# Three-layer graph network with routed feed-forward on one core: surplus pass reordered by its dependences, a second bank for the layer product, and the norm taken tile by tile

## What is computed

```
norm = deg[src]**-0.5 * deg[dst]**-0.5      # edges and self loops
h = layernorm(x)                            # x: 6250 x 256, fp32
for W, b in three layers:
    h = segment_sum((h @ W)[src] * norm, dst) + b     # relu after the first two
x = x + h
n = layernorm(x);  r = n @ wr + br
out = x + n
chosen = the 3124 of 6250 rows with the highest r
out[chosen] += r[chosen] * (gelu(n[chosen] @ w1 + b1) @ w2 + b2)
```

## Time and profile before

| | |
|---|---|
| three runs | 2053.6, 2049.27, 2052.75 us, median 2052.75 |
| profiled execution | 2062.73 us, span 2061.0 us |
| mean granted TensorE clock | 0.959 of full |
| PE busy | 1861.0 us of the span, 90% |
| first sum of layer 2 / of layer 3 (DVE) | 964 us / 1464 us |
| end of the last unit | 1858.6 us |
| PE's last matmul ends | 2051.7 us |

### The profile page before, as it was taken

One profiled execution on the slowest core, in us unless ns is written; L12 is line 12 of the kernel. 1 busy time (PEld: TensorE's weight loads), 2 busy tenths in 40 slices (PEclk: granted clock), 3 DMA queues, 4 the chain that ended last, 5 costly groups with the idle time before them and its releaser, 6 DMA issues.

```text
span 2061.0 us, 28897 instructions
## 1 busy us (share of the span) xinstructions
PE 1861.0 (90%) x10168; PEld 1068.9 (52%) x10168; DVE 1054.3 (51%) x3267; ACT 528.7 (26%) x1126; POOL 1161.9 (56%) x1213
## 2 busy tenths in 40 slices
PE   6874789998899999988999999998899989999898
PEld 5762456665555556543445554544444434446665
DVE  7877688886566566631222221210345444786422
ACT  5824134333344455510211111110000000002120
POOL 5400674666676667523677777762477767762211
PEclk9965899999999999999999999999999999999999
DMA  7649143544455556574667766764588869854200
GB/s 255 195 168 306 40 153 122 178 152 153 158 196 184 178 196 208 193 266 146 212 224 242 239 229 224 233 238 154 205 301 306 308 214 332 312 183 145 63 24 24
DMA packets 170597, 405.02 MB, mean 197 GB/s; under 512 B 29436, under 2 KB 122546, under 8 KB 157657
## 3 DMA queue, kind: packets, MB, share of 16 engines
q1 hardware_dynamic: 119864, 265.05, 36.4%
q0 software_dynamic: 50592, 138.13, 21.2%
HBM read 284.18 MB, written 118.89 MB: 196 GB/s over the span
## 4 chain that ended last, share of the span: by engine, by line
PE 67%; POOL 10%; issue 9%; DVE 7%; DMA 5%; ACT 2%; POOLq 0%; DVEq 0%; ACTq 0%
PE ag L1246 21%; PE pw L1246 16%; PE ag L1258 9%; POOL space_rows L1835 6%; PE pw L1214 5%; PE both L1272 4%; PE pw L1340 3%; PE ag L1353 2%; PE pw L1353 2%; PE ag L1340 1%; PE both L1264 1%; POOL space_rows L1802 1%; POOL space_rows L1827 1%; DMA space_rows<-row_dram,src_s 1%; DMA extra<-space_tables 1%
## 5 line engine op out<-in xcount | busy, mean ns | idle before, releaser
L1835 POOL DMA_INDIRECT space_rows<-row_dram,src_s x947 | 967.9, 1022 | 378.7 <-issue 207.7
L1246 PE MATMUL ag<-space_a,space_ring 128*128 128x512 f16 x2107 | 628.9, 382 | 30.5 <-POOL space_ring L1843 30.5
L1214 PE MATMUL pw<-space_tables 128*128 128x147 f16 (+1 forms) x2022 | 330.1, 248 | 51.5 <-DVE space_tables L871 43.0
L1258 PE MATMUL ag<-space_rows,hots 128*128 128x512 f16 x947 | 359.6, 380 | 5.1 <-DMA space_rows<-row_dram,src_s 3.3
L1214 PEld LDWEIGHTS pw<-space_tables 128*128 128x128 f16 x2022 | 218.9, 116 | 238.5 <-DVE space_tables L871 68.8
L871 DVE TENSOR_TENSOR space_tables<-iota_two,space_tables 128x294 f16<-128x294 f16 (+1 forms) x1011 | 306.6, 338 | 0.0
L1582 ACT ACTIVATE space_ring<-pw 128x784 f16<-128x784 f32 (+1 forms) x257 | 220.1, 857 | 312.3 <-PE pw L1214 308.5
L1246 PEld LDWEIGHTS ag<-space_a,space_ring 128*128 128x128 f16 x2107 | 198.9, 98 | 133.5 <-issue 27.3
L868 DVE TENSOR_TENSOR space_tables<-iota_many,space_tables 128x512 f16<-128x512 f16 x506 | 215.2, 425 | 59.1 <-PE pw L1214 56.5
L1246 PE MATMUL pw<-space_b,space_ring 128*128 128x512 f16 x784 | 204.4, 381 | 6.4 <-DVE space_work L895 6.4
L1246 PE MATMUL pw<-space_a,space_ring 128*128 128x512 f16 x686 | 172.0, 381 | 1.9 <-DVE space_b L895 1.9
(11 more groups left out here) (407 smaller groups left out, 1926.8 us busy)
## 6 DMA issues: line engine op xcount, KB each, us to landing
space_ring<-adj SPq DMA_DIRECT2D x49, 1568.0 KB, 7.5
adj<-space_ring SPq DMA_DIRECT2D x34, 1568.0 KB, 6.2
space_tables<-adj SPq DMA_DIRECT2D x17, 1568.0 KB
extra<-hots SPq DMA_DIRECT2D x3, 6272.0 KB, 23.2
space_work<-extra SPq DMA_DIRECT2D x147, 128.0 KB
space_rows<-row_dram,src_s POOLq DMA_INDIRECT x947, 3.7
space_b<-in_x_turned SPq DMA_DIRECT2D x7, 896.0 KB, 13.6
space_a<-in_x SPq DMA_DIRECT2D x7, 896.0 KB, 5.4
```

Of the source, the lines that this page charges most:

```text
L1214: pe.matmul(pw[v % 2][:, half, at_c:at_c + n], olo[:, j % RING // 2, :, j % 2 * 2 + i], ohi[:, j % RING, 0:n, i], start=s == FIRST[w], sto ...
L1246: mm = pe.matmul(bank(q), a[:, k, :], hh[l][:, k, :], start=i == 0 and not own, stop=i == TILES - 1)
L1258: pe.matmul(bank(q), hots_area[:, hot_at, :, g - SPOT_GROUPS[SPOT_GROUP_OF[g]][0]], slots[g % GR], start=False, stop=i == n).then_inc(g_us ...
L1835: pool.indirect_dma_start(slots[g % GR], None, row_dram[STEP_LAYER[g]], bass.IndirectOffsetOnAxis(src_s[:, s:s + 1], 0)).then_inc(g_in[g % ...
```

## The change

- `spill`: the edges are requested, then the target index is computed and the old sum requested with a semaphore of its own (`old_in`); then the wait for the edges, the wait for `rows_out[l]`, the request of the source rows (`more_rows_in`), and the one-hot computed after that. Behind ACT's copy POOL waits only for `old_in`.
- The 8 row steps ahead of `spill(1)` and `spill(2)` are fetched behind them. `SPILL_AT` of these stands 20 units earlier, `OVER_AT` (and with it the first sums of a layer) 30 units earlier.
- The product of layers two to three goes into `pw[1][:, 1]`; its turns wait for ACT's copy of the tile before (`relued`), no more for `lo_s`.
- The norm's statistics are taken with each sum; variance at `NORM_AT`, reciprocal 4 units later, tile i of the group at 6(i+1) units behind `NORM_AT`. `aggr` and `rstd_x` have two buffers.
- The last group of four tiles becomes one of three and one of one; the one tile has an own slot of `xn`.
- Phase two of the choice: the turns' settles stand ahead of its begin, its steps start 3 places earlier at a spacing of 3.8 instead of 4, and the turns of the second block stand one step earlier.

```
 LAG = 5
-AHEAD = 8
...
 BN = 6
-NORMS = (7, 7, 7, 7, 5, 5, 7, 4)
+NORMS = (7, 7, 7, 7, 5, 5, 7, 3, 1)
...
 END = [max(u for u, (p, i) in enumerate(UNIT) if p == q) + 1 for q in range(len(Q))]
-SPILL_AT = [END[0], START[TILES] + 170, START[2 * TILES] + 170]
-OVER_AT = [SPILL_AT[0] + 45, SPILL_AT[1] + 60, SPILL_AT[2] + 60]
+SPILL_AT = [END[0], START[TILES] + 150, START[2 * TILES] + 150]
+OVER_AT = [SPILL_AT[0] + 45, SPILL_AT[1] + 50, SPILL_AT[2] + 50]
...
 SPOTS = by_unit([STEP_UNIT[a] - 60 for a, b in SPOT_GROUPS])
+NORM_SPACE = 6
+XN_FROM = [0] * (len(NORMS) - 1) + [NORMS[-2]]
+NORM_TILE = [(g, i) for g, n in enumerate(NORMS) for i in range(n)]
+NORM_TILE_AT = [NORM_AT[g] + NORM_SPACE * (i + 1) if g < len(NORMS) - 1 else NORM_AT[g] for g, i in NORM_TILE]
+NORM_TILES_OF = by_unit(NORM_TILE_AT)
+ROOTED_OF = by_unit([u + 4 if g < len(NORMS) - 1 else u for g, u in enumerate(NORM_AT)])
...
 def turn_places():
-    hidden = {(0, 4 + i): [s] for i, s in enumerate(BLOCKS[1])} | {(SECOND, 2 + i): [s] for i, s in enumerate(BLOCKS[SECOND + 1])}
+    hidden = {(0, 3 + i): [s] for i, s in enumerate(BLOCKS[1])} | {(SECOND, 2 + i): [s] for i, s in enumerate(BLOCKS[SECOND + 1])}
...
-CHOICE_BEGINS, CHOICE_SPACE = 17.0, 4.0
+CHOICE_BEGINS, CHOICE_SPACE = 14.0, 3.8
...
     both = ps("both", [P, 2 * D])
-    px, ph = both[:, 0:D], both[:, D:2 * D]
+    px = both[:, 0:D]
+    ph = [both[:, D:2 * D], pw[1][:, 1, 0:D]]
...
+            def spread_of_tile(k):
+                (g, i), t = NORM_TILE[k], Q[2 * TILES + k]
+                chained(dve.bn_stats(stats[:, i, :], nodes[:, t]))
+                chained(dve.bn_aggr(aggr[:, g % 2, i, :], stats[:, i, :]))
+
+            def spread_of_group(g):
                 n = NORMS[g]
...
+                chained(dve.tensor_scalar(rstd_x[:, g % 2, 0:n], aggr[:, g % 2, 0:n, 1], EPS, None, ALU.add))
+                steps[f"spread {g}"] = done_x["n"]
+
+            def rooted_group(g):
+                n = NORMS[g]
+                dve.wait_ge(root_s, g + 1)
+                chained(dve.reciprocal(rstd_x[:, g % 2, 0:n], rstd_x[:, g % 2, 0:n]))
+
+            def norm_tile(k):
+                (g, i), t = NORM_TILE[k], Q[2 * TILES + k]
+                if i == 0 and 0 < g <= EARLY_GROUPS:
+                    dve.wait_ge(pairs_out, 48 * NORM_FROM[g])
+                elif i == 0 and g and not XN_FROM[g]:
+                    dve.wait_ge(pairs_late, 48 * (NORM_FROM[g] - EARLY))
+                to = xn[:, XN_FROM[g] + i]
+                chained(dve.tensor_scalar(to, nodes[:, t], aggr[:, g % 2, i, 0:1], rstd_x[:, g % 2, i:i + 1], ALU.subtract, ALU.mult))
+                dve.tensor_tensor(nodes[:, t], nodes[:, t], to, ALU.add).then_inc(norm_s, 1)
+                dve.scalar_tensor_tensor(x_junk, to, 1.0, wr_b, ALU.mult, ALU.mult, accum_out=route[:, t:t + 1]).then_inc(stat_s, 1)
+                done_x["n"] += 1
+
+            def begin_choice(ph):
                 dve.wait_ge(stat_s, done_x["n"])
...
                             add_x(q)
+                            spread_of_tile(q - 2 * TILES)
                     for g in NORMS_OF.get(u, ()):
-                        norm_group(g)
-                        if g == EARLY_GROUPS - 1:
+                        spread_of_group(g)
+                    for g in ROOTED_OF.get(u, ()):
+                        rooted_group(g)
+                    for k in NORM_TILES_OF.get(u, ()):
+                        norm_tile(k)
+                        if k == EARLY - 1:
...
             upto(UNITS + 300)
+            hidden_turns(0)
             begin_choice(1)
-            for c in range(len(BLOCKS) + 1):
+            for c in range(1, len(BLOCKS) + 1):
                 if c < len(BLOCKS) and c != SECOND:
                     hidden_turns(c)
-                for s in BLOCKS[c - 1] if c else ():
+                for s in BLOCKS[c - 1]:
                     weigh(s)
-                for s in BLOCKS[c - 1] if c else ():
+                for s in BLOCKS[c - 1]:
...
                 pe.wait_ge(summed, q + 1)
-                pe.wait_ge(lo_s, q)
+                pe.wait_ge(lo_s, min(q, TILES))
+                if q > TILES:
+                    pe.wait_ge(relued, q)
...
                 for f in range(HALVES):
-                    mm = pe.matmul(ph[:, 0:D], fresh[:, q % 2, f, :], gw_sb[:, l, f, :], start=f == 0, stop=f == HALVES - 1)
+                    mm = pe.matmul(ph[l - 1], fresh[:, q % 2, f, :], gw_sb[:, l, f, :], start=f == 0, stop=f == HALVES - 1)
...
+            def landed(name):
+                pool.wait_ge(name, 16)
+                pool.inc_swdge_sem([name], [16], mode="sub")
+                pool.sem_inc(passed, 1)
+
             def moved(ins):
                 ins.then_inc(more_in, 16)
-                pool.wait_ge(more_in, 16)
-                pool.inc_swdge_sem([more_in], [16], mode="sub")
-                pool.sem_inc(passed, 1)
+                landed(more_in)
...
                         each(pool.tensor_scalar(edge_i, edge, float(E), None, ALU.min))
-                        moved(pool.indirect_dma_start(pair_i, None, edges, bass.IndirectOffsetOnAxis(edge_i, 0)))
+                        pool.indirect_dma_start(pair_i, None, edges, bass.IndirectOffsetOnAxis(edge_i, 0)).then_inc(more_in, 16)
+                        each(pool.tensor_tensor(base_of, item[:, 1:2], part_f[:], ALU.add))
+                        each(pool.tensor_copy(target_i, base_of))
+                        if l < 0:
+                            pool.wait_ge(deg_clear, 16)
+                        else:
+                            pool.wait_ge((stored_0, stored_s, stored_s)[l], 32 if l else 16)
+                        pool.indirect_dma_start(more_old[:, 0:width], None, target,
+                                                bass.IndirectOffsetOnAxis(target_i, 0)).then_inc(old_in, 16)
+                        landed(more_in)
+                        if l >= 0:
+                            pool.wait_ge(rows_out[l], 16 * (TILES if l else GROUPS))
+                            pool.indirect_dma_start(more_rows, None, row_dram[l],
+                                                    bass.IndirectOffsetOnAxis(pair_i[:, 1:2], 0)).then_inc(more_rows_in, 16)
                         each(pool.tensor_copy(node, pair_i[:, 0:1]))
...
                         each(pool.tensor_scalar(more_hot, iota16[:, 0:P], node, None, ALU.is_equal))
-                        each(pool.tensor_tensor(base_of, item[:, 1:2], part_f[:], ALU.add))
-                        each(pool.tensor_copy(target_i, base_of))
                         if l >= 0:
-                            moved(pool.indirect_dma_start(more_rows, None, row_dram[l],
-                                                          bass.IndirectOffsetOnAxis(pair_i[:, 1:2], 0)))
+                            landed(more_rows_in)
                         pool.sem_inc(more_ready, 1)
                         pool.wait_ge(more_out, pool.snap(n))
                         pool.sem_inc(passed, 1)
-                        if l < 0:
-                            pool.wait_ge(deg_clear, 16)
-                        moved(pool.indirect_dma_start(more_old[:, 0:width], None, target,
-                                                      bass.IndirectOffsetOnAxis(target_i, 0)))
+                        landed(old_in)
...
             add_loops(0)
-            pool.wait_ge(rows_out[0], 16 * GROUPS)
-            pool.wait_ge(stored_0, 16)
...
             for l in range(1, 3):
-                pool.wait_ge(rows_out[l], 16 * TILES)
-                for g in range(LAYER_STEP[l], LAYER_STEP[l] + AHEAD):
-                    fetch_row(g)
-                if l == 1:
-                    pool.wait_ge(stored_s, 32)
                 spill(l)
...
                     pool.partition_all_reduce(small[:, 19:20], small[:, 18:19], P, RED.max).then_inc(m_p, 1)
-                for g in range(LAYER_STEP[l] + AHEAD, LAYER_STEP[l + 1]):
+                for g in range(LAYER_STEP[l], LAYER_STEP[l + 1]):
...
                     sp.wait_ge(norm_s, NORM_FROM[g] + i + 1)
-                    sp.dma_start(pair_dram[t * P:t * P + P, 0:D], xn[:, i]).then_inc(stored, 16)
+                    sp.dma_start(pair_dram[t * P:t * P + P, 0:D], xn[:, XN_FROM[g] + i]).then_inc(stored, 16)
```

40 lines of the change are left out of this document (5 added, 35 removed).

## The result

| | before | changed |
|---|---|---|
| median of the runs | 2053.18 us (4 runs, 2049.27 to 2054.44) | 2026.28 us (4 runs, 2023.74 to 2033.52) |
| profiled execution, its span | 2062.73, 2061.0 us | 2023.98, 2022.2 us |
| ratio | | 0.9878, interval 0.9847 to 0.9909 |

The change makes the kernel 26.9 us faster (the interval goes from 19 to 31), 8 us less than the forecast of 35, and 2026.28 lies inside the forecast range of 1998 to 2038.

The account below looks back on a forecast made before the run. PE, busy 90% of the span, was taken as the bound, so gains came from its 200 us idle. Terms summed to 35.3 us; against the median 2052.75 that gave 2017.5, rounded to 2018 us, range 1998 to 2038.

Parts of the forecast that it names:

- Degree pass: Start of the kernel: POOL fetches old degrees earlier, so the add starts 3.2 us sooner; gain 3.2 us.
- Surplus pass of layer 1: PE's 13.3 us wait there shortens because the surplus rows are requested sooner, behind the slow POOL add; gain 3.0 us.
- The sign I gave: Layer 1: one PE wait near 10 us for the surplus pass, with the long POOL add still there.
- Layers 1 to 2: Surplus pass ready before PE comes, all-reduce earlier, 2.0 us wait and most of the 6.40 gone; gain 10.1 us.
- The bank: Layer 2: 14 turn waits for DVE's product go, six of them given back to POOL's row pace; gain 7.8 us.
- the sign that the prediction gave for itself: The forecast is wrong if, among other signs, PE's waits for rows exceed 5 us in sum.
- Layers 2 to 3: The 8.9 us surplus-pass wait goes, with a 1.88 us wait and about 0.9 us of clock; gain 11.7 us.
- Norm in pieces: Layer 3: the next sum stands behind two norm tiles, no longer behind a whole group of seven; gain 13.4 us.
- The tail, against: DVE waits for group 6's 21 stores ahead of the settles, so a PE turn waits 15.8 us; loss 17.1 us.
- The tail, for: One-tile last group and phase two one output block ahead, with 4.9 us of settle wait left; gain 3.2 us.
- The rival that rows take gains back: POOL's row fetches take back the bank's gain and half the norm's: 2033 us, chance 14%.
- The rival of DVE's pieces blocking POOL: Layer 3: norm pieces delay POOL's row fetches, making the kernel slower; 2067 us at 0.2 us a step, chance 4%.

Follow-up runs that it names:

- second looks: Kernel before and changed kernel, each profiled a second time with no edit: 2048.57 us and 2027.78 us, one time each.
- experiment 5: Changed kernel with the surplus pass, its place in the unit order and the eight row fetches ahead of it as before: 2047.34 us.
- experiment 9: Changed kernel with late norm tiles behind the settles, plus layer 2's first surplus sums fetched 6 units earlier, ahead of an adjacency load: 2010.36 us.
- Experiments 2, 3 and 8: Changed kernel, in that order: product in its old bank, 2026.47 us; layer 2 row fetches halved to 64 rows, 2009.53 us; both together, 2023.64 us.
- Experiment 1: Changed kernel with the three norm tiles of the group before last moved behind the four settles and the last sum: 2010.06 us.

## Why the prediction was right, and where it was not

**Degree pass: failed.** 3.2 us forecast, none found. I took DVE's 7.94 us of standing still for a wait on POOL's pass, and 3.2 us as the gain. The pass did end sooner (SP fetched the degrees at 154.39 in place of 157.19), and the first dense step still came no earlier, at 206.9 and 205.5 before and 207.9 in both looks after. PE's turn of the degrees had no idle time ahead of it in the trace of before:

```profile
157.53 3.59 PE L1493 MATMUL ag<-degs,space_rows 16*128 16x15 f32 x16
161.06 0.93 PE L1214 MATMUL pw<-space_tables 128*128 128x147 f16 x6
161.91 0.66 PE L1500 MATMUL ag<-ident,by_tile 49*128 49x49 f32 x2
```

PE was busy with its own list until it reached that turn. The step that failed was naming the releaser's releaser without looking at it.

**Surplus pass of layer 1: right.** 3.0 us forecast; the wait went from 13.3 to 9.6, in the second looks from 13.2 to 11.05, and the stretch to matmul 150 got 4.3 and 6.3 us shorter (2.2 against experiment 5, which has the old pass). The sign I gave, the long POOL add still there, held in the second look; in the first it was the edge request that was held.

**Layers 1 to 2: right in mechanism, a term too large.** 10.1 for the pass and 4.9 for the first five waits of the bank make 15.0; measured 13.0 (89.6 to 76.6) at matmul 2250. But 4.6 of these lie behind the first sparse step and are given back. Up to that step, with the pass and the three waits of the bank ahead of it (10.1 + 2.9 = 13.0 forecast), PE gained 8.5 and 8.4 us. I had 0.4 us of the wait left where 3.2 stayed. The turn now stands 30 units earlier, ahead of the point I had priced, and the surplus sums wait in SP's queue behind a load (experiment 9).

**The bank: the term that failed.** I counted five waits before 997 and the last three behind 1310 as kept, 7.8 us, and took only the six between as given back. The pace of the rows starts earlier, at POOL's 17th fetch (987.16), and lasts to the end of the layer. Only the three waits ahead of it (2.9 us) count in full; the other 11 (10.6 us) brought 2.2 and 1.3 us between the first and the last sparse step. PE came to that stretch earlier and waited for rows in it instead, 12.3 us for 3.3 in the whole kernel. That the stage of layer 2 got 3.9 us longer (3.2 between the second looks) is the same thing seen from matmul 2250: the 4.6 us that PE was ahead there were given back. By the sign that the prediction gave for itself it was wrong here: rows were to wait no more than 5 us in sum, and they waited 12.3. Experiments 2, 3 and 8 show the mechanism: with fetches 0.04 us closer the stage is 12.6 to 15 us shorter, and then the bank's waits in it cost 6.2 us.

**Layers 2 to 3: right.** 11.7 forecast, 12.5 and 11.6 measured.

**Norm in pieces: right.** 13.4 forecast; 3.0 + 10.6 = 13.6 measured in the two stages (2.7 + 10.6 between the second looks). Behind it 1.6 to 2.6 us are lost again to rows, which I had kept only in the range.

**The tail, against: right.** A wait of 15.8 us forecast, 15.84 and 14.14 measured; DVE's wait for the stores about 10, 10.41 measured. The granted clock in the 7 us behind it was 0.81, so 1.3 us and not 2.0:

```profile
1815.00:1822.00 7.00, 7.00 (x29) 3.63 (x30) 1.35 (x4) 0.00 (x0) 0.00 (x0) 0.81 0.24 77
```

**The tail, for: right.** I found 4.9 us left at phase two; 2.81 + 1.87 = 4.7 were. Experiment 1, where the new wait is gone, leaves 1.9 to 4.0 us of gain in the stretch; 3.2 was forecast. Both parts together were to cost 13.9; the stretch to the end is 14.2 us longer, 11.0 between the second looks.

**The sum.** 35.3 forecast and 26.9 measured. The gap is more than made up by two places: the degree pass, 3.2 forecast and none found, and matmul 1950 to 3900, 17.9 forecast and 9.1 found (9.6 between the second looks). By the traces the forecast was further off than by the medians: without the dense part of layer 1, which the change doesn't touch, the two pairs of traces lie 23.0 and 24.5 us apart. That agrees with 26.9 only because the interval is 6 us to either side, so how close the total came is in part luck; the wide range covers both. The rival that rows take gains back named the right mechanism; at 2033 it also took half of the norm's gain, which stayed. The rival of DVE's pieces blocking POOL didn't come: the usual spacing of the fetches in layers 2 and 3 stayed 1.25 us.

## What to carry to other kernels

A wait in front of a shared resource can sit ahead of work that has nothing to do with it: before moving an operation earlier on an in-order engine, list what is queued behind its slowest wait. Here one line that put three norm tiles behind four copies was worth 16 us. When one engine feeds another at a fixed pace, find the moment at which the pace starts (here the first use of a full ring): a wait removed ahead of it lasts, one behind it is mostly given back. Price the pace first, since 0.04 us a fetch was worth 12.6 to 15 us and the 14 removed waits 6.6 to 7.5. And look at the releaser's own idle time before counting a gain through it.
